# A graph-attention and expert kernel: a wait on GpSimd, a running sum moved off VectorE, filler matmuls and a different set-up

## The chip, the cores and the metric

The kernel runs on one core of one Trainium2 chip. The core's engines are TensorE (PE in the rows; PEld is its weight load), VectorE (DVE), ScalarE (ACT), GpSimd (POOL) and SyncE (SP, which issues the DMAs). The time is device microseconds of one execution; lower is better. Three runs of the kernel before took 2379.27, 2380.46 and 2383.46 us, so the median is 2380.46 us.

## What is computed

The input x is 128 graphs of 128 nodes and 256 features. Layer one is graph attention, layer two a dense mixture of eight experts whose gate is the mean over all graphs:

```python
x = x + gnn(layernorm(x), adj, W, a)
x = x + ffn(layernorm(x), Wr, br, W1, ..., Wo, bo)

# gnn
Wh = h @ W;  s1 = Wh @ a[:256];  s2 = Wh @ a[256:]
e = leaky_relu(s1[:, :, None] + s2[:, None, :], 0.2) + log(adj + 1e-6)
h_prime = softmax(e, axis=-1) @ Wh

# ffn
w = softmax(mean(x, axis=0) @ Wr + br)
h = relu(bn(x @ W1 + b1));  h = relu(bn(h @ W2 + b2));  y = h @ Wo + bo
out = einsum('bfed,fe->bfd', y, w)
```

All of it is fp32; the expert products are three matmuls each on operands split into a high and a low part.

## The kernel before

**Two stages in two blocks.** The graph stage works on G = 32 groups of GB = 4 graphs, one group per step of a software pipeline that every engine walks through in its own loop. In step g, PE projects group g (L716, `project`), the attention of group a = g-1 is computed, and the result x1 of group b = g-2 is formed. The seam is where the graph stage ends and the block of the expert stage begins; the expert stage then runs 256 units (32 tiles by 8 experts) on PE.

**Steps and their kinds.** Steps 0 to 5 and 30 to 33 are written out. Steps 6 to 21 (`layer == 1`) also prepare the W1 weights: in an even step POOL forms four sums in `w_stage` (L451 to L458), in an odd step ACT makes `wq_hi` (L520) and POOL `wq_lo` (L463). Steps 22 to 29 (`layer == 2`) prepare W2: ACT `w_hi` (L532), POOL `w_lo` (L468).

**One step, engine by engine.** DVE: `l_sb` (L621), the row maximum `neg_m` (L628), x1 of group b (L646), the weights p of group a (L658), then eight `bn_stats` (L574, L582). ACT: `s_sb` (L506), its share of the running sum (L514), `wq_hi` in odd steps, `e_sb` (L526), `wh` of group g (L541), which needs POOL's `dev`, then `pT` (L557) and `xnT` (L562). POOL: weight work, its share of the running sum (L476), then `deviations` of the next group (L404 to L424), which needs the `bn_stats` of DVE and whose last instruction is a power that yields `dev`. Each engine executes its list in order.

**The gate's running sum** `acc` (the tile `resb`) adds x1 times its rstd for every group. Of the four graphs of a group h = g-4, DVE adds the two lower (`add_part`, L608); for the two upper ACT writes the scaled copy `x1s_high` (L514) and POOL adds it (L476). There is one `x1s_high` buffer, so ACT's copies of group h wait for POOL's addition of group h-1 (`wait(act, acc_high_done, num(h))`, L512).

**Set-up.** PE transposes the first x tile, forms the column mean of the projection weights `gw` (L694), transposes gw and the vector a (L701, L702), and multiplies them (L708) to append two columns to gw; ACT copies between these steps (L493 to L496). The projection of group 0 waits for that.

**The seam and the end.** `tile_normalise` of tile 0 (L124) stands in step 30 ahead of x1; the three `tile_low` (L162) stand in step 32. In the second block DVE takes the statistics of group 31 (L1029, L1033) and adds groups 30 and 31 to acc (L179). The last tile's output is stored by one DMA of 512 KB (L905).

## Time and profile before

| | us |
|---|---|
| median of three runs | 2380.46 |
| the profiled execution, its own time | 2380.82 |
| its span | 2379.0 |
| set-up to the first `l_sb` (step 1) | 23.19 |
| steps 6 to 21 | 124.90 |
| steps 22 to 29 | 64.03 |
| step 30 to the first matmul of the second block | 29.1 |
| expert stage, first matmul to the end | 2098.7 |

Rows of the timeline give the start, the duration, engine, line, operation, tiles written and read, and in brackets the idle time ahead of the instruction and what ended it. Where several instructions are merged in one row, the duration is that of all. Consecutive instructions overlap a little, so the spacing of starts (called pitch below) says more than a duration.

### The profile page before, as it was taken

The numbers are of one execution on the slowest core, as the hardware profiler recorded it, in microseconds if no ns is written. First come the engines' busy times: TensorE is split into PE (matmuls) and PEld (weight loads), VectorE is DVE, ScalarE is ACT, GpSimd is POOL, SyncE is SP. The second block draws the span as 40 slices with busy tenths as digits, with TensorE's granted clock in tenths as the row PEclk, the third lists the DMA queues.
The fourth block names the chain that finished last, engine by engine and source line by source line (L and its number), as shares of the span: only waits on it lengthen the run. The fifth ranks groups of instructions, "written<-read, shape, count | busy, mean of one in ns | idle before, by whom it ended". The sixth has DMA issues, their size and how long they took to land.

```text
span 2379.0 us, 46022 instructions
## 1 busy us (share of the span) xinstructions
PE 2339.6 (98%) x16164; PEld 2166.8 (91%) x16164; DVE 1687.8 (71%) x2577; ACT 1615.7 (68%) x2524; POOL 435.0 (18%) x566
## 2 busy tenths in 40 slices
PE   8999799999999999999999999999999999999999
PEld 7777689999999999999999999999999999999998
DVE  5999866666776766676666676666666666677666
ACT  5888676666666666666666666666666666666665
POOL 4898621111101011111111101011111111001010
PEclk9999799999999999999999999999999999999999
DMA  5778410000000000000000000000000000000000
GB/s 175 255 251 267 154 36 27 27 26 26 26 26 25 19 9 26 26 26 26 26 26 26 26 26 18 20 14 26 26 26 26 26 26 26 26 26 18 18 10 27
DMA packets 91178, 116.16 MB, mean 49 GB/s; under 512 B 4700, under 2 KB 78856, under 8 KB 91144
## 3 DMA queue, kind: packets, MB, share of 16 engines
q1 hardware_dynamic: 91144, 115.73, 14.8%
q8 instruction: 19, 0.31, 0.1%
q14 instruction: 15, 0.12, 0.0%
HBM read 82.16 MB, written 33.55 MB: 49 GB/s over the span
## 4 chain that ended last, share of the span: by engine, by line
PE 88%; DVE 0%; ACT 0%; issue 0%
PE ps_y L1174 31%; PE ps_wide L171 30%; PE ps_wide L1155 26%; PE ps_t L132 1%; DVE h_lo L1059 0%; DVE z L1052 0%; ACT h_hi L954 0%; ACT v L959 0%; DVE resb L1082 0%; DVE h_lo L1065 0%; DVE z L1042 0%; PE ps_t L1219 0%; PE ps_t L1201 0%; PE ps_t L1206 0%; ACT featT L985 0%
## 5 line engine op out<-in xcount | busy, mean ns | idle before, releaser
L959 ACT ACTIVATE v<-ps_wide,bn_cols 128x256 f32<-128x256 f32 x768 | 434.1, 565 | 375.0 <-PE ps_wide L1155 245.1
L967 ACT ACTIVATE h<-ps_wide,bn_cols 128x512 f32<-128x512 f32 x512 | 399.2, 780 | 314.2 <-PE ps_wide L171 312.0
L1174 PE MATMUL ps_y<-wo_hi,h_hi 128*128 128x256 f32 x2048 | 579.3, 283 | 0.5 <-DVE h_lo L1065 0.5
L1174 PE MATMUL ps_y<-wo_lo,h_hi 128*128 128x256 f32 x2048 | 579.6, 283 | 0.0
L1174 PE MATMUL ps_y<-wo_hi,h_lo 128*128 128x256 f32 x2048 | 579.5, 283 | 0.0
L1059 DVE SCALAR_TENSOR_TENSOR h_lo<-z,h_hi 128x1024 fp32r<-128x1024 f32 x256 | 313.8, 1226 | 341.6 <-ACT h_hi L954 341.6
L1155 PE MATMUL ps_wide<-xq_hi,wq_hi 128*128 128x256 f32 x1792 | 500.9, 279 | 7.4 <-PEq L185 3.1
L1155 PE MATMUL ps_wide<-xq_lo,wq_hi 128*128 128x256 f32 x1792 | 497.8, 278 | 0.0
L1155 PE MATMUL ps_wide<-xq_hi,wq_lo 128*128 128x256 f32 x1792 | 497.0, 277 | 0.0
L171 PE MATMUL ps_wide<-h_hi,w_lo 128*128 128x512 f32 x1024 | 403.9, 394 | 0.0
L171 PE MATMUL ps_wide<-h_lo,w_hi 128*128 128x512 f32 x1024 | 402.0, 393 | 0.0
L171 PE MATMUL ps_wide<-h_hi,w_hi 128*128 128x512 f32 x1024 | 398.3, 389 | 0.5 <-DVE h_lo L1059 0.5
L1174 PEld LDWEIGHTS ps_y<-wo_hi,h_lo 128*128 128x128 f32 x2048 | 392.5, 192 | 0.0
L1174 PEld LDWEIGHTS ps_y<-wo_hi,h_hi 128*128 128x128 f32 x2048 | 390.4, 191 | 1.1 <-DVE h_lo L1065 0.7
L1174 PEld LDWEIGHTS ps_y<-wo_lo,h_hi 128*128 128x128 f32 x2048 | 390.6, 191 | 0.0
L1065 DVE TENSOR_TENSOR h_lo<-h,h_hi 128x1024 fp32r<-128x1024 f32 x256 | 313.5, 1225 | 85.3 <-ACT h_hi L973 82.1
L938 POOL TENSOR_TENSOR resb<-resb,w_bc 128x512 f32<-128x512 f32 x64 | 85.4, 1336 | 1543.4 <-DMA resb<-x_scratch 1537.4
L1155 PEld LDWEIGHTS ps_wide<-xq_hi,wq_hi 128*128 128x128 f32 x1792 | 340.1, 190 | 19.0 <-issue 3.8
L1155 PEld LDWEIGHTS ps_wide<-xq_hi,wq_lo 128*128 128x128 f32 x1792 | 338.4, 189 | 9.8
L1155 PEld LDWEIGHTS ps_wide<-xq_lo,wq_hi 128*128 128x128 f32 x1792 | 338.2, 189 | 0.0
L1082 DVE SCALAR_TENSOR_TENSOR resb<-ps_y,w_node,resb 128x512 f32<-128x512 f32 x448 | 333.3, 744 | 3.9 <-PE ps_y L1174 3.9
L1052 DVE SCALAR_TENSOR_TENSOR z<-ps_wide,bn_cols,v 128x512 f32<-128x512 f32 x256 | 191.9, 750 | 153.4 <-PE ps_wide L1155 145.9
(131 smaller groups left out, 2995.6 us busy)
## 6 DMA issues: line engine op xcount, KB each, us to landing
x_sb<-in_x SPq DMA_DIRECT2D x32, 512.0 KB, 4.0
res<-in_x SPq DMA_DIRECT2D x32, 512.0 KB, 5.9
x1t<-x_scratch SPq DMA_DIRECT2D x32, 512.0 KB, 3.2
resb<-x_scratch SPq DMA_DIRECT2D x32, 512.0 KB, 3.2
out<-resb SPq DMA_DIRECT2D x32, 512.0 KB, 2.9
adj_sb<-in_adj SPq DMA_DIRECT2D x32, 256.0 KB, 6.1
x_scratch<-h SPq DMA_DIRECT2D x16, 512.0 KB, 4.7
x_scratch<-w_bc SPq DMA_DIRECT2D x16, 512.0 KB, 4.9
```

Of the source, the lines that this page charges most:

```text
L132: last = nc.tensor.transpose(ps_x[:, c, b4 * N:(b4 + 1) * N], x1t[:, b4, c * P:(c + 1) * P], ident[:, :])
L171: mm = nc.tensor.matmul(acc_ps, w[:, i, c, cols], s[:, c, :], start=start and n == 0, stop=stop and n == len(terms) - 1)
L938: nc.gpsimd.tensor_tensor(resb[:, g, :], resb[:, g, :], ysum[:, g, :], ALU.add).then_inc(resb_done, 1)
L959: nc.scalar.activation(v[:, slot, :], ps_l1[:, 0, 0:H], ACT.Identity, bias=bn_cols[:, 1, cols], scale=bn_cols[:, 0, cols]).then_inc(done, 1)
L967: nc.scalar.activation(h2[:, m, :], ps_l2[:, m, :], ACT.Relu, bias=bn_cols[:, 3, cols], scale=bn_cols[:, 2, cols]).then_inc(r2_done, 1)
L1052: nc.vector.scalar_tensor_tensor(out=z[:, 0, :], in0=ps_l1[:, 1, :], scalar=bn_cols[:, 0, C * e:C * e + 1], in1=v[:, 0:2, :].rearrange("p ...
L1059: nc.vector.scalar_tensor_tensor(out=h1_lo[:, :, :], in0=z[:, :, :], scalar=0.0, in1=h1_hi[:, :, :].bitcast(F32), op0=ALU.max, op1=ALU.sub ...
L1065: nc.vector.tensor_tensor(h2_lo[u[1] % 2][:, :, :], h2[:, :, :], h2_hi[u[1] % 2][:, :, :].bitcast(F32), ALU.subtract).then_inc(lo2_done, 1)
L1082: nc.vector.scalar_tensor_tensor(out=dst[:, g, :], in0=ps_y[:, g, :], scalar=w_node[:, e:e + 1], in1=old, op0=ALU.mult, op1=ALU.add).then_ ...
L1155: mm = nc.tensor.matmul(out_ps, w[:, e, q, :], x[:, q, :], start=start and n == 0, stop=stop and n == len(terms) - 1, skip_group_check=True)
L1174: mm = nc.tensor.matmul(ps_y[:, b4, :], h[:, c, cols], w[:, e, c, :], start=(k == 0 and b4 % per_bank == 0), stop=(k == len(terms) - 1 and ...
```

## The change

- POOL waits for both halves of p of group a (`p_done`) at the start of each step, ahead of its weight work and its addition.
- The running sum: ACT scales all four graphs of group h into `x1s` (four activations, where there were two), POOL adds 128x1024 in one instruction (128x512 before), DVE's two additions are gone. The order of buffers stays: ACT's copies of group h wait for POOL's addition of h-1 (`acc_done_a`). Groups 30 and 31 are still added by DVE in the second block, now both in `feature_mean`, and their statistics are both taken there.
- `tile_normalise` of tile 0 moves behind p in step 30; the third `tile_low` moves to step 33; `deviations` of step 32 is dropped.
- Set-up: a is loaded broadcast over the partitions; DVE forms gw times a with four accumulating instructions instead of PE's transposes; seven matmuls are issued ahead of the first transpose; an Exp is issued early on ACT.
- Filler matmuls (`keep_clock`): 5 in step 32, 4 in step 33, and 6, 12, 6 and 6 in the first three units of the second block.
- The last tile is stored in two halves.

```diff
                 def step(g, layer):
+                    a = ago(g, 1)
+                    if exists(a):
+                        pool.wait_ge(p_done, 2 * num(a) + 2)
                     if layer == 1 and g[1] == 0:
...
-                        pool.wait_ge(x1s_high_done, num(h) + 1)
-                        wait(pool, acc_high_done, num(h))
-                        nc.gpsimd.tensor_tensor(acc[:, HB:, :], acc[:, HB:, :], x1s_high[:, :, :],
-                                                ALU.add).then_inc(acc_high_done, 1)
+                        pool.wait_ge(x1s_done, num(h) + 1)
+                        pool.wait_ge(acc_set, 1)
+                        wait(pool, acc_done_a, num(h))
+                        nc.gpsimd.tensor_tensor(acc[:, :, :], acc[:, :, :], x1s[:, :, :],
+                                                ALU.add).then_inc(acc_done_a, 1)
...
                         act.wait_ge(dev_done, num(h) + 4)
-                        wait(act, acc_high_done, num(h))
-                        for b4 in range(HB, GB):
-                            last = nc.scalar.activation(x1s_high[:, b4 - HB, :], x1[h[1]][:, b4, :], ACT.Copy,
+                        wait(act, acc_done_a, num(h))
+                        for b4 in range(GB):
+                            last = nc.scalar.activation(x1s[:, b4, :], x1[h[1]][:, b4, :], ACT.Copy,
                                                         scale=rstd_all[:, num(h), b4:b4 + 1])
...
-                    add_part(0)
-                    add_part(1)
...
+                dve.wait_ge(proj_loaded, 2 * 16)
+                for c in range(C):
+                    for k in range(2):
+                        last = nc.vector.scalar_tensor_tensor(
+                            out=x1t[:, 2 * c + k, :], in0=gw[:, c, 0:D], scalar=1.0, in1=a_bc[:, k, :], op0=ALU.mult,
+                            op1=ALU.mult, accum_out=gw[:, c, D + k:D + k + 1])
...
+                    if is_step(g, G):
+                        pe.wait_ge(wh_copied, G)
+                        keep_clock(5)
...
+                    if starts(new, 0) or starts(new, 1) or starts(new, 2):
+                        keep_clock(6)
...
+                    if starts(new, 0):
+                        keep_clock(12)
...
                 def feature_mean():
+                    dve.wait_ge(last_rstd_done, 1)
+                    add_group(G - 2)
                     dve.wait_ge(acc_done, 1)
```

**How the lists read.** POOL in an odd step of the W1 loop, before: the low part of W1, the half addition, the first deviation.

```order
L463 ISA [waits wq_hi_done]
L463 TENSOR_TENSOR wq_lo<-w_stage,wq_hi 128x896
L474 REGISTER_ALU
L476 TENSOR_TENSOR resb<-resb,x1s_high 128x512 [waits acc_high_done,x1s_high_done]
L400 ISA
L402 REGISTER_ALU [waits bnst1]
L404 TENSOR_TENSOR dif<-st 128x8 [waits dev_done,bnst2]
```

The same place in the changed kernel.

```order
L459 ISA [waits wq_hi_done,p_done]
L459 TENSOR_TENSOR wq_lo<-w_stage,wq_hi 128x896
L470 REGISTER_ALU
L473 TENSOR_TENSOR resb<-resb,x1s 128x1024 [waits acc_done_a,acc_set,x1s_done]
L393 ISA
L395 REGISTER_ALU [waits bnst1]
L397 TENSOR_TENSOR dif<-st 128x8 [waits dev_done,bnst2]
```

A wait for p stands ahead of the weight work, and the addition has twice the columns; nothing changed places.

ACT in the same odd step, before: the scaled copies, the high part of W1, the exponentials.

```order
L514 ISA [waits acc_high_done]
L514 ACTIVATE x1s_high<-w_bc,dev 128x256
L514 ISA
L514 ACTIVATE x1s_high<-w_bc,dev 128x256
L519 REGISTER_ALU
L520 ISA [waits wq_sum]
L520 ACTIVATE wq_hi<-w_stage 128x896
L526 ACTIVATE e_sb<-l_sb,neg_m 128x128 [waits p_done,neg_m_done]
```

And in the changed kernel.

```order
L506 ISA [waits acc_done_a]
L506 ACTIVATE x1s<-w_bc,dev 128x256
L506 ISA
L506 ACTIVATE x1s<-w_bc,dev 128x256
L506 ISA
L506 ACTIVATE x1s<-w_bc,dev 128x256
L506 ISA
L506 ACTIVATE x1s<-w_bc,dev 128x256
L511 REGISTER_ALU
L512 ISA [waits wq_sum]
L512 ACTIVATE wq_hi<-w_stage 128x896
L518 ACTIVATE e_sb<-l_sb,neg_m 128x128 [waits p_done,neg_m_done]
```

Four copies now stand between the wait for POOL's addition and the exponentials.

PE in the set-up, before: from the first transposes to the projection of group 0.

```order
L685 MATMUL ps_th<-ident,x_sb 128x128 x7
L694 MATMUL ps_wide<-gw,mean_w 128x256 [waits proj_loaded,mean_w_set]
L694 MATMUL ps_wide<-gw,mean_w 128x256
L701 MATMUL ps_wide<-ident,gw 128x128 [waits gw_centred]
L701 MATMUL ps_wide<-ident,gw 128x128 x3
L702 MATMUL ps_s<-ident,a_rows 128x4
L708 MATMUL ps_s<-a_cols,gwT 128x2 [waits proj_T_copied]
L708 MATMUL ps_s<-a_cols,gwT 128x2 x3
L716 MATMUL ps_wide<-gw,xnT 128x258 [waits xnT_copied,va_copied]
```

And in the changed kernel.

```order
L675 MATMUL ps_th<-ident,x_sb 128x128 x7
L686 MATMUL ps_wide<-gw,mean_w 128x256 [waits proj_loaded]
L686 MATMUL ps_wide<-gw,mean_w 128x256
L691 MATMUL ps_wide<-gw,mean_w 128x2 [waits va_ready]
L691 MATMUL ps_wide<-gw,mean_w 128x2
L704 MATMUL ps_wide<-gw,xnT 128x258 [waits xnT_copied,gw_centred]
```

The transposes of gw and a and the eight small products are gone; two narrow products of the mean stand in their place.

## Rows read from the trace of the kernel before

**Rows 1.** The page: busy time, share of the span and instructions of each engine.

```profile
PE 2339.6 (98%) x16164; PEld 2166.8 (91%) x16164; DVE 1687.8 (71%) x2577; ACT 1615.7 (68%) x2524; POOL 435.0 (18%) x566
```

**Rows 2.** Busy time by stage: stretch, length, busy us of each engine, clock, DMA.

```profile
0.00:23.19 23.19, 15.60 (x68) 12.57 (x69) 3.31 (x9) 7.14 (x16) 5.81 (x23) 1.00 0.42 130
62.25:187.15 124.90, 118.75 (x641) 99.14 (x640) 122.53 (x400) 106.34 (x281) 112.24 (x183) 1.00 0.77 250
187.15:251.18 64.03, 59.05 (x321) 49.88 (x320) 61.74 (x201) 53.73 (x145) 50.48 (x79) 1.00 0.86 279
251.18:280.31 29.13, 19.91 (x94) 15.32 (x93) 27.44 (x80) 17.55 (x46) 22.55 (x39) 0.87 0.33 111
280.31:298.87 18.56, 15.08 (x58) 12.84 (x58) 12.12 (x26) 8.09 (x13) 6.30 (x8) 0.56 0.32 104
```

**Rows 3.** Timeline, DVE, an even and an odd step of the W1 loop.

```profile
114.66 1.38 DVE L582 BATCH_NORM_STATS2 st<-h 128x6 f32<-128x256 f32 x4
115.97 0.86 DVE L608 SCALAR_TENSOR_TENSOR resb<-w_bc,dev,resb 128x256 f32<-128x256 f32 x2
116.75 0.68 DVE L621 SCALAR_TENSOR_TENSOR l_sb<-s_sb 128x512 f32<-128x512 f32 x1
...
119.63 0.28 DVE L658 SCALAR_TENSOR_TENSOR p_sb<-adj_sb,e_sb 128x128 f32<-128x128 f32 x1
...
120.27 0.29 DVE L658 SCALAR_TENSOR_TENSOR p_sb<-adj_sb,e_sb 128x128 f32<-128x128 f32 x1
```

**Rows 4.** Timeline, ACT, the odd step that begins at 116.75.

```profile
116.40 0.95 ACT L514 ACTIVATE x1s_high<-w_bc,dev 128x256 f32<-128x256 f32 x2
117.20 0.99 ACT L520 ACTIVATE wq_hi<-w_stage 128x896 f32 x1
118.19 1.28 ACT L526 ACTIVATE e_sb<-l_sb,neg_m 128x128 f32<-128x128 f32 x4
120.50 1.58 ACT L541 ACTIVATE wh<-ps_wide,dev 128x258 f32<-128x258 f32 x4 [1.04 <-POOL dev L424]
```

**Rows 5.** Timeline, POOL, the same two steps.

```profile
113.81 0.46 POOL L458 TENSOR_TENSOR w_stage<-w_stage 128x128 f32<-128x128 f32 x1
114.23 1.27 POOL L476 TENSOR_TENSOR resb<-resb,x1s_high 128x512 f32<-128x512 f32 x1
116.21 0.30 POOL L404 TENSOR_TENSOR dif<-st 128x8 f32<-128x8 f32 x1 [0.71 <-DVE st L582]
...
118.72 1.65 POOL L424 TENSOR_TENSOR dev<-ve,minus_half 128x8 f32 x1 [0.19 <-POOL ve L420]
120.33 2.17 POOL L463 TENSOR_TENSOR wq_lo<-w_stage,wq_hi 128x896 f32 x1
122.47 1.26 POOL L476 TENSOR_TENSOR resb<-resb,x1s_high 128x512 f32<-128x512 f32 x1
123.70 0.39 POOL L404 TENSOR_TENSOR dif<-st 128x8 f32<-128x8 f32 x1
```

**Rows 6.** Timeline, DVE and POOL in step 31, where p and the addition meet.

```profile
263.94 1.28 POOL L476 TENSOR_TENSOR resb<-resb,x1s_high 128x512 f32<-128x512 f32 x1
...
263.98 1.38 DVE L658 SCALAR_TENSOR_TENSOR p_sb<-adj_sb,e_sb 128x128 f32<-128x128 f32 x1
```

**Rows 7.** Timeline: centring on DVE, projection of group 0, one of a later step.

```profile
8.05 0.69 DVE L587 SCALAR_TENSOR_TENSOR gw<-gw,ps_wide 128x512 f32<-128x512 f32 x1 [8.05 <-PE ps_wide L694]
...
12.99 5.52 PE L716 MATMUL ps_wide<-gw,xnT 128*128 128x258 f32 x16 [0.26 <-ACT gw L496]
...
116.92 3.65 PE L716 MATMUL ps_wide<-gw,xnT 128*128 128x258 f32 x16
```

**Rows 8.** Timeline, step 30: the normalisation on DVE, a small POOL instruction beside it.

```profile
252.50 1.38 DVE L124 TENSOR_SCALAR x1t<-x1t,mean_all,dev 128x256 f32<-128x256 f32 x4
252.60 0.36 POOL L417 TENSOR_TENSOR mean_all<-two_means,half_cols 128x4 f32 x1
```

**Rows 9.** Timeline, the end: the one store of the last tile.

```profile
2375.70 0.40 SPq L905 DMA_DIRECT2D out<-resb  x1
```

168 lines of the change are left out of this document (89 added, 79 removed).

## The prediction

> **What bounds the kernel now.** I read the page first: PE is busy for 98% of the span [rows 1]. That is the expert stage, which the change leaves alone apart from its first three units and its last store. So whatever the change is worth, it is worth in the first 299 us, and there I read the busy time by stage [rows 2]. From step 6 to step 21, the steps that prepare W1, DVE is busy 122.53 us of 124.90, but POOL also 112.24 and ACT 106.34. Eight pairs of steps in 124.90 us make 15.61 us a pair. A full row is not proof of a bound, so I then went through one pair on the timeline to see which wait ends last. In the odd step ACT's wh stands idle for 1.04 us for POOL's dev [rows 4], and POOL itself goes from dev straight on into wq_lo and the addition, with no gap between rows [rows 5]. POOL's only rest in the pair is 0.71 us. So in these steps DVE and POOL share the bound, and work that is taken from DVE and given to POOL is not free.
>
> **What the change buys there.** DVE loses its two additions; they take 0.78 us of a step (start at 115.97, next at 116.75) [rows 3]. The wait for p removes collisions: in step 31 the addition starts at 263.94, and the last p, which elsewhere takes 0.29 us [rows 3], takes 1.38 us, until POOL is done [rows 6]. So a POOL instruction that holds the shared port keeps a two-input DVE instruction out for its whole length, and one such hit costs 1.1 us. Behind p stand bn_stats, which the POOL rows do not disturb (four in 1.38 us beside the addition at 114.23) [rows 3, 5].
>
> [...]
>
> **What it costs there: a loop of waits.** There is one x1s buffer. ACT may copy group h only when POOL has added group h-1. Behind the copies ACT has, in order, wq_hi and then e_sb; e_sb releases p on DVE; and now p releases POOL, which does its weight work and only then the next addition. Before, the last link was missing: POOL took up weight work without p. Now each addition depends on the one before through all of this, once a step. Its links:
> - POOL's end to ACT's start, 0.13 us (dev ends at 120.37, wh starts at 120.50) [rows 4, 5];
> - four copies. Two take 0.80 (116.40 to 117.20) [rows 4], so four take 1.60;
> - wq_hi, odd steps only, 0.99 [rows 4];
> - e_sb 1.28 [rows 4], and 0.10 to DVE (between 0 and the 0.16 that lie between its end and p) [rows 3, 4];
> - p 0.93, from 119.63 to the end of the last at 120.56 [rows 3];
> - DVE to POOL 0.17 (bn_stats end at 116.04, dif starts at 116.21) [rows 3, 5];
> - POOL's weight work: wq_lo 2.14 from start to start [rows 5]; in even steps four sums at a pitch of 0.42 [rows 5], two with a wait for the one before, for which I add 0.13 each: 1.94;
> - the addition of 1024 columns. 512 take 1.23, 896 (wq_lo) take 2.14 [rows 5], 2.37 ns a column between them, so 2.44; doubling gives 2.46.
>
> Odd: 0.13 + 1.60 + 0.99 + 1.28 + 0.10 + 0.93 + 0.17 + 2.14 + 2.44 = 9.78 us. Even: the same without 0.99 and with 1.94 for 2.14, 8.59 us. The pair is 18.37 us against 15.61: +2.76, and over eight pairs +22.1. The first step enters without an addition to wait for by some 0.4 us, so I take **+21.7 us**. l_sb cannot escape: it has two SBUF inputs, and the addition holds the port until its end. The gains above are inside this sum, for it counts p clean and no DVE addition.
>
> [...]
>
> **Steps 22 to 29.** POOL has w_lo there, 512 columns, as long as the old addition, 1.23, and w_hi stands behind e_sb on ACT. The loop is 0.13 + 1.60 + 1.28 + 0.10 + 0.93 + 0.17 + 1.23 + 2.44 = 7.88 us, against 64.03 / 8 = 8.00 [rows 2]. The other chain, dev to wh to xnT to s_sb to l_sb, is about as long; I take **-0.6** (bounds -3 and +1). **Steps 4 and 5** have no weight work, the loop is 6.65, under the 6.9 that DVE needs for a step without its addition (122.53 / 16 - 0.78) [rows 2, 3]: they lose one collision of 1.1 [rows 6] and give 0.1 back, **-1.0**.
>
> **Step 30 to the end of the graph stage.** The normalisation (1.38 us in four instructions) now follows p, where POOL's addition starts. Beside it, before, a POOL instruction of four columns took 0.36 [rows 8], more than the eight-column dif beside DVE's addition, 0.30 [rows 5], so the two do contend. I expect one of the four to run and three to wait the addition out: 2.4 us lost, where 1.1 was lost to a p collision and some 0.3 to DVE's addition. **+1.0** (bounds -1.5, no contention, and +1.5). Behind that POOL has two additions with four copies between, 2.44 + 0.13 + 1.60 + 0.17 + 2.44 = 6.8 us, in place of two half additions and a dropped round of deviations of about 7; but the tile's sums start behind a full addition: **+0.6** (0 to +1.5). Five fillers in step 32 may save that step's slow matmuls; POOL ends later anyway.
>
> **Set-up.** Now the centring ends at 8.74 and the projection starts at 12.99 [rows 7]. Of these 4.25 us a narrow product and a narrow DVE instruction remain, for which I take 0.65 (dif is 0.30 to 0.39, and two signals) [rows 5]: -3.6. The accumulating products fit before the column mean is there at 8.05. The projection takes 5.52 where 3.65 is usual [rows 7]; the earlier matmuls may bring the clock up: between 0 and -1.9, I take the middle. **-4.5** (bounds -2.5 and -6). The cover is the load of a; if its broadcast lands late, that comes off.
>
> **Second block.** [...] Fillers can bring the clock up sooner, but feature_mean now adds two groups in front of unit 1's z: four more instructions at 0.39 [rows 3], +1.6 on DVE's path, which then ends last. **-0.7** (bounds -4, and +2.7 if 24 fillers at 0.26, the mean of 15.08 / 58 [rows 2], fill 3.5 of idle and push the rest). **The last store** takes 3.3 us from its issue to the span's end [rows 9]; half the bytes after the last instruction save **-0.7** (0 to -1.2).
>
> **The sum** is 21.7 - 0.6 - 1.0 + 1.0 + 0.6 - 4.5 - 0.7 - 0.7 = +15.8 us. The profiled execution took 2380.82 us, 0.4 above the median of three. So 2396 us.
>
> **Rivals.**
> - *The loop does not close, POOL's own load decides.* If ACT's copies are never late, POOL's work per pair remains: 1.94 + 2.14 + 4.88 + twice 3.8 for deviations (116.21 to 120.37 is 4.16 [rows 5], less what DVE's addition blocked) = 16.6. +7.6 in place of +21.7: 2382. For it: the copies stand early in ACT's list. Against: the addition ends after they are due.
> - *The port is the whole story (faster).* If l_sb and bn_stats fit around the addition, a step falls toward DVE's own 6.9; I take 7.5, since ACT's list is longer now, so 15.0 a pair: -4.9, all in all 2380.8 - 5.9 - 4.9 = 2370. The place is the addition behind p: it decides once addition and weight work end within the 2.6 us of bn_stats (twice 114.66 to 115.97) [rows 3]. The addition alone fits; with weight work it does not, on rows.
> - *The loop and the losses at the edges*: fillers on a slow clock, the tail's blocked instructions: 2401 to 2403.
>
> **How the numbers follow.** The loop as summed 0.68, the loop with losses 0.10, POOL's load alone 0.12, faster 0.10. The range reaches from the third case's edge, 2382, to 2403. A measurement of this kernel tells about 0.2%, 4.8 us, from no change: faster 0.10, same 0.10, slower 0.80.
>
> **What would show it.** Between step 6's and step 22's l_sb some 146 us in place of 124.90. In an odd step: copies start 0.1 to 0.2 us after an addition ends, e_sb waits for nothing but ACT itself, p starts right behind e_sb, POOL is idle before wq_lo with p as releaser, and l_sb lasts long or starts as the addition ends. Wrong if the addition takes well under 2.3 us, or if the pair stays at 15.6. The set-up is right if the first l_sb starts near 18.7, step 30 if the normalisation's four instructions are stretched to some 3.7 us.

## The result, and where the time is found in the profile after

The changed kernel takes **2436.65 us** (median of 4 runs, 2435.42 to 2439.39) against 2379.94 of the kernel before, measured with it: ratio 1.0237, 95% interval 1.0219 to 1.0255. It is slower by 56.7 us; forecast were 2396 us and a range of 2382 to 2403. The sign was right, the size was not.

Busy time by stage of the changed kernel, with the same borders as [rows 2] (the starts of l_sb in steps 1, 6, 22 and 30, the second block's first product, unit 1's last z). Columns: stretch, length, busy us of PE, PEld, DVE, ACT and POOL with their instructions, granted clock, DMA share, GB/s.

```profile
0.00:17.76 17.76, 13.32 (x73) 11.31 (x74) 5.01 (x18) 6.51 (x14) 5.86 (x22) 1.00 0.65 182
17.76:55.53 37.77, 35.84 (x196) 30.03 (x195) 29.59 (x106) 30.03 (x84) 23.70 (x43) 1.00 0.67 217
55.53:200.29 144.76, 120.40 (x641) 98.77 (x641) 120.09 (x368) 118.13 (x312) 119.00 (x181) 1.00 0.66 216
200.29:268.09 67.80, 60.80 (x321) 49.23 (x321) 55.20 (x184) 59.74 (x160) 56.16 (x81) 1.00 0.81 263
268.09:298.75 30.66, 22.35 (x113) 17.71 (x112) 26.10 (x69) 20.81 (x54) 21.98 (x33) 1.00 0.35 113
298.75:317.65 18.90, 14.49 (x80) 12.49 (x81) 12.85 (x26) 7.99 (x13) 8.56 (x13) 0.86 0.38 118
```

In the profiled executions the span went from 2379.0 to 2433.6 us, +54.6. Stage by stage:

| stage | before | after | difference | the sum had |
|---|---|---|---|---|
| set-up, to step 1's l_sb | 23.19 | 17.76 | -5.4 | -4.5 |
| steps 1 to 6 | 39.06 | 37.77 | -1.3 | -1.0 |
| steps 6 to 22 (W1) | 124.90 | 144.76 | **+19.9** | +21.7 |
| steps 22 to 30 (W2) | 64.03 | 67.80 | **+3.8** | -0.6 |
| step 30 to the second block | 29.16 | 30.66 | +1.5 | +1.6 |
| second block to unit 1's last z | 17.73 | 18.89 | +1.2 | -0.7 |
| from there to the end | 2080.94 | 2115.95 | **+35.0** | -0.7 |

The last line is the surprise: the expert stage, in which the change edits nothing. Here is one tile of its loop, from the first product (one matmul instruction) behind the transposes to the same product of the next tile, first in the kernel before, then in the changed one:

```profile
1030.39:1095.39 65.00, 65.00 (x467) 61.01 (x466) 44.83 (x55) 43.75 (x62) 6.66 (x7) 1.00 0.07 24
```

```profile
1063.26:1129.35 66.09, 66.09 (x468) 61.67 (x465) 44.83 (x55) 43.76 (x62) 6.82 (x7) 1.00 0.07 24
```

Same products, same granted clock (1.00, the upper of the two levels in these traces; the lower is 0.50), PE without a gap in both, DVE and ACT busy as long as before, and yet 1.09 us more per tile. So each product must take longer from start to start. Timeline of PE, a run of 12 products of layer 1 and the first of layer 3, before:

```profile
1023.71 0.28 PE L1155 MATMUL ps_wide<-xq_hi,wq_hi 128*128 128x256 f32 x1
...
1024.96 0.28 PE L1155 MATMUL ps_wide<-xq_lo,wq_hi 128*128 128x256 f32 x1
1025.07 0.28 PE L1174 MATMUL ps_y<-wo_hi,h_hi 128*128 128x256 f32 x1
```

and the same run in the changed kernel:

```profile
1065.48 0.28 PE L1172 MATMUL ps_wide<-xq_hi,wq_hi 128*128 128x256 f32 x1
...
1066.79 0.28 PE L1172 MATMUL ps_wide<-xq_lo,wq_hi 128*128 128x256 f32 x1
1066.91 0.27 PE L1196 MATMUL ps_y<-wo_hi,h_hi 128*128 128x256 f32 x1
```

12 products take 1.36 us before and 1.43 after: 113 against 119 ns. The column of durations (0.28 in both) hides it, since products overlap; only the starts show it. Layers 1, 2 and 3 are the expert's products x W1, h W2 and h Wo. Added up from each product's start to the next one's, and averaged over the tiles of the loop in whose records nothing is missing, the time of a tile by layer is:

| us a tile | layer 1 (168 products, 256 columns) | layer 2 (96, 512 columns) | layer 3 (192, 256 columns) | period |
|---|---|---|---|---|
| before | 19.20 | 21.97 | 23.03 | 65.00 |
| after | 20.09 | 22.38 | 22.84 | 66.09 |

Before, layer 1 is at 113 ns product after product (at 118 in part of the unit behind the transposes). After, it runs through a cycle: 122, 120, 119, 115, 117, 122, 120, ... Behind the first few tiles the same figures recur in every tile, to within a nanosecond. (The transposes and a few small products make up the other 0.79 us of the period, in both kernels.)

**The loop of waits in W1.** Two steps of the changed kernel, l_sb at 145.31 and 154.63: POOL, ACT and DVE apart.

```profile
144.30 2.36 POOL L473 TENSOR_TENSOR resb<-resb,x1s 128x1024 f32<-128x1024 f32 x1
...
151.29 0.46 POOL L447 TENSOR_TENSOR w_stage<-w_stage 128x128 f32<-128x128 f32 x1 [0.98 <-DVE p_sb L642]
...
153.20 2.36 POOL L473 TENSOR_TENSOR resb<-resb,x1s 128x1024 f32<-128x1024 f32 x1
...
160.59 2.10 POOL L459 TENSOR_TENSOR wq_lo<-w_stage,wq_hi 128x896 f32 x1 [1.37 <-DVE p_sb L642]
162.64 2.35 POOL L473 TENSOR_TENSOR resb<-resb,x1s 128x1024 f32<-128x1024 f32 x1
```

```profile
146.87 1.71 ACT L506 ACTIVATE x1s<-h,dev 128x256 f32<-128x256 f32 x4 [1.68 <-POOL resb L473]
148.48 1.26 ACT L518 ACTIVATE e_sb<-l_sb,neg_m 128x128 f32<-128x128 f32 x4
...
155.71 1.71 ACT L506 ACTIVATE x1s<-w_bc,dev 128x256 f32<-128x256 f32 x4 [1.11 <-POOL resb L473]
157.32 0.94 ACT L512 ACTIVATE wq_hi<-w_stage 128x896 f32 x1
158.16 1.26 ACT L518 ACTIVATE e_sb<-l_sb,neg_m 128x128 f32<-128x128 f32 x4
```

```profile
145.31 1.90 DVE L611 SCALAR_TENSOR_TENSOR l_sb<-s_sb 128x512 f32<-128x512 f32 x1 [0.64 <-ACT s_sb L498]
...
148.61 1.66 DVE L630 SCALAR_TENSOR_TENSOR h<-ps_th,rinv,res 128x256 f32<-128x256 f32 x4 [0.67 <-ACT x1s L506]
150.19 0.28 DVE L642 SCALAR_TENSOR_TENSOR p_sb<-adj_sb,e_sb 128x128 f32<-128x128 f32 x1
...
159.45 0.29 DVE L642 SCALAR_TENSOR_TENSOR p_sb<-adj_sb,e_sb 128x128 f32<-128x128 f32 x1 [0.24 <-ACT e_sb L518]
```

The loop closes as forecast: the copies wait 1.68 and 1.11 us for POOL's addition, POOL waits 0.98 and 1.37 us for p, and works through its weight work before the next addition. From step to step l_sb starts 9.31 and 9.01 us apart, 18.32 a pair (forecast: 18.37). One link is not in the forecast: x1 (L630) waits 0.67 us for the copies, "<-ACT x1s". In the odd round p starts behind e_sb (0.24 us of waiting). In the even one it starts behind x1, at 150.19, when e_sb has been done since 149.74: there the path goes through x1 and not through e_sb.

### The profile page after: what moved, and what is told of

It reads as the page before. It is cut to its first block, busy times and chain, and to the rows that moved or that the text cites. A ratio compares the mean times of both kernels' runs of the same rounds, so it can differ in the third digit from the quotient of the medians.

```text
span 2433.6 us, 46080 instructions
## 1 busy us (share of the span) xinstructions
PE 2378.8 (98%) x16217; PEld 2188.9 (90%) x16217; DVE 1677.2 (69%) x2522; ACT 1638.5 (67%) x2582; POOL 450.7 (19%) x562
## 4 chain that ended last, share of the span: by engine, by line
PE 88%; POOL 3%; DVE 3%; ACT 2%; issue 2%; DMA 0%; ACTq 0%; DVEq 0%; POOLq 0%; SPq 0%
PE ps_y L1196 30%; PE ps_wide L168 29%; PE ps_wide L1172 26%; POOL resb L473 2%; ACT x1s L506 1%; PE ps_t L129 1%; DVE p_sb L642 1%; DVE st L566 1%; PE ps_wide L704 1%; DVE h L630 0%; ACT e_sb L518 0%; PE ps_th L721 0%; ACT wq_hi L512 0%; DVE w_bc L630 0%; DMA w_stage<-in_L_ffn_Wo 0%
## 5 line engine op out<-in xcount | busy, mean ns | idle before, releaser
L1172 PE MATMUL ps_wide<-xq_hi,wq_hi 128*128 128x256 f32 x1792 | 510.4, 285 | 7.1 <-DVE z L1058 3.4
L1172 PE MATMUL ps_wide<-xq_hi,wq_lo 128*128 128x256 f32 x1792 | 506.5, 283 | 0.0
L1172 PE MATMUL ps_wide<-xq_lo,wq_hi 128*128 128x256 f32 x1792 | 506.2, 282 | 0.0
L168 PE MATMUL ps_wide<-h_hi,w_hi 128*128 128x512 f32 x1024 | 404.5, 395 | 0.6 <-DVE h_lo L1075 0.6
L1172 PEld LDWEIGHTS ps_wide<-xq_hi,wq_hi 128*128 128x128 f32 x1792 | 340.1, 190 | 19.4 <-DVE z L1058 4.1
```

The source lines that it names most:

```text
L168: mm = nc.tensor.matmul(acc_ps, w[:, i, c, cols], s[:, c, :], start=start and n == 0, stop=stop and n == len(terms) - 1)
L1172: mm = nc.tensor.matmul(out_ps, w[:, e, q, :], x[:, q, :], start=start and n == 0, stop=stop and n == len(terms) - 1, skip_group_check=True)
```

## The experiments

The first question is the expert stage. In the changed kernel ones_cols is gone, last_st has grown and last_mv is gone. All that is allocated behind them lies elsewhere: by the author's estimate wq and w 32 bytes lower, w_bc, h2, x1t, xs and xq 32 bytes higher, h1, h2_hi, h2_lo and wo 192 bytes higher. No profile shows an address, and how much room a buffer of 16 bytes takes was not shown: the places in bytes, here and in the expectations, are that estimate, made from the sizes of the buffers. The first theory is that these places cost the time. The rival is something else in the changed program.

**Moving buffers only.** The edit of `a1_before_off64` to the kernel before (nothing reads or writes the three buffers; by the estimate wq, w and xq then lie against a multiple of 64 bytes as they do in the changed kernel):

```diff
+        pad_w = sb("pad_w", [P, GB])
         wq_hi = sb("wq_hi", [P, E, Q, P], F32R)
...
+            pad_a = sba("pad_a", [P, GB])
             bn_rows = sba("bn_rows", [EC, 2, 5, P])
...
+            pad_b = sbb("pad_b", [P, GB])
             last_ve = sbb("last_ve", [P, GB])
```

> [...] Theory A (the start address of an operand costs TensorE time): the tile period rises from 65.00 to about 66.1 us and the whole by 30 to 34 us, to about 2412. Theory B (something else in the changed kernel, such as where its instructions lie, makes the expert stage slower): period 65.0, time 2380. No theory expects a change before step 32.

Measured: 2411.25 us (2410.14 to 2412.49), ratio 1.0131, interval 1.0114 to 1.0148. Period 65.99, and the graph stage is the same (W1 124.75, second block at 279.89). So 31 us come from the places of buffers alone.

`a2_after_on64` puts the same three lines into the changed kernel (pad_b ahead of last_dif):

> The changed kernel with nothing changed but the same three unused buffers, so that wq, w, xq, h1 and wo all start on multiples of 64 bytes again, as in the kernel before. Theory A: the tile period falls from 66.09 to 65.0 us and the whole to about 2404, which leaves +24 us from the first 320 us. Theory B: 66.1 and 2437.

Measured: 2436.58 us, ratio 1.0240 (1.0223 to 1.0257), period 66.11. No time came back. Either theory A was wrong in the changed kernel, or a multiple of 64 is not the condition.

`a3_after_weights_on64` has the changed kernel with

```diff
+        pad_w = sb("pad_w", [P, GB])
         wq_hi = sb("wq_hi", [P, E, Q, P], F32R)
...
+        pad_s = sb("pad_s", [P, GB])
         last_st = sb("last_st", [P, 2, GB, 6])
```

> The changed kernel with one unused buffer ahead of wq_hi and one ahead of last_st: the weights wq and w start on multiples of 64 bytes, w_bc, h2, resb, x1t, xs and xq stay 32 bytes off. Layer 2 (weights w, activations h1, which are aligned in both kernels) slowed down too, from 228.8 to 232.9 ns, so within theory A the weights are the likelier side: period 65.0, time about 2404. If it is the streamed activations alone: period about 65.4 to 66.1. Theory B: 66.1 and 2437.

and `a4_after_acts_on64` with

```diff
+        pad_x = sb("pad_x", [P, GB])
         w_bc = sb("w_bc", [P, E, P])
```

beside pad_a and pad_b:

> The changed kernel with one unused buffer ahead of w_bc (and the two at the starts of stage A's and the second block's buffers): w_bc, h2, resb, x1t, xs and xq start on multiples of 64 bytes, the weights wq and w stay 32 bytes off. Theory A with the weights as the side that counts: period 66.1, time 2437. With the streamed activations: layer 1 fast again, about 65.4 (the 144 products of 120 columns by 5 ns less) and 2414, layer 2 as slow as in the changed kernel. Theory B: 66.1 and 2437.

Measured: a3 2420.81 us (ratio 1.0175), a4 2437.52 us (1.0245). In a3 layer 2 is back at 21.96 us a tile, layer 1 still at 20.00; a4 moved little (20.01 and 22.52). a4 (66.15 us a tile) came out as forecast for the weights as the side that counts, and for theory B; a3 (65.63) as forecast for the streamed side alone. No one theory fitted both, so the next kernel put everything back.

**The changed kernel with its buffers where they were.**

```diff
+        pad_w = sb("pad_w", [P, GB])
         wq_hi = sb("wq_hi", [P, E, Q, P], F32R)
...
-        last_st = sb("last_st", [P, 2, GB, 6])
+        pad_s = sb("pad_s", [P, 32])
...
         xq_lo = sb("xq_lo", [P, Q, H], F32R)
+        last_st = sb("last_st", [P, 2, GB, 6])
...
+            pad_a = sba("pad_a", [P, 88])
...
+            pad_b = sbb("pad_b", [P, 40])
```

> The changed kernel with its buffers put back where the kernel before has them: wq, w, w_stage, w_bc, h2, resb, x1t, xs and xq at exactly the same addresses (an unused buffer of 16 bytes where ones_cols was, one of 128 bytes where last_st and last_mv were, last_st itself behind xq_lo), h1, h2_hi, h2_lo and wo of the second block 512 bytes above theirs, stage A's x_sb, xnT and p_sb at theirs. Theory A2 (TensorE's pitch depends on where the operands lie, by more than a multiple of 64): layer 1 again at a constant 113 ns, period 65.00, time 2403 to 2405. Theory B (something else of the changed kernel makes the expert stage slower, and the moved buffers of the first four runs only added to that): period 66 and 2434 to 2438. Steps 6 to 22 stay at 144.8 us by both.

Measured: **2400.76 us** (2400.59 to 2402.93), ratio 1.0092 (1.0075 to 1.0109). W1 is 144.77 us, and one tile is

```profile
1051.06:1116.06 65.00, 65.00 (x467) 61.01 (x466) 44.84 (x55) 43.75 (x62) 6.57 (x7) 1.00 0.07 24
```

as before, with the three layers at 19.20, 21.97 and 23.03 us. That settles it: 36 us of the 57 come from where the buffers lie, and none of these from the program's instructions. What is left, 20.7 us, is the change proper.

`b2_before_acts_64_up` moves, in the kernel before, xq and its neighbours by 64 bytes (pad_x of 16 columns ahead of w_bc, pad_a and pad_b of 112):

> The kernel before with the weights in place and w_bc, h2, resb, x1t, xs and xq 64 bytes higher (still multiples of 64, but no longer of 128); the second block's buffers 512 bytes higher. If the multiple of 128 of the streamed xq, or its distance from wq, is what keeps layer 1 at 113 ns: layer 1 rises to 118 to 120 ns, the period by 0.8 to 1.0 us (168 products by 5 to 6 ns), the time to 2404 to 2410. If only the multiple of 64 counts: 65.00 and 2380.

Measured: 2414.67 us, ratio 1.0150 (1.0133 to 1.0167), period 66.11, with the three layers at 20.08, 22.21 and 23.03 us, the very figures of a2. By the sizes of the buffers the two kernels agree in where wq, w and xq lie, and in h1, h2 and wo to a multiple of 256 bytes: the same places, two different programs, the same pitches. The kernel before lost 35 us because xq and the buffers allocated with it moved by 64 bytes, from one multiple of 64 to the next. (The second block's buffers moved by 512 bytes as well, as they did in b1, which lost nothing by it.) Layer 2 rose by 0.24 us a tile although neither w nor h1 moved against a multiple of 512: a layer's pitch is not decided by its own operands alone.

**The products alone.** `m1_places_alone` has TensorE with nothing beside it:

```diff
+            def product(bank, w, x, n, start, stop):
+                return nc.tensor.matmul(ps[:, bank, 0:n], wa[:, w:w + P], xa[:, x:x + n], start=start, stop=stop)
+
+            def layer_1(sw, sx, k):
+                for q in range(k):
+                    r = q % 7
+                    for w, x in ((0, 0), (7168, 0), (0, 1792)):
+                        last = product(0, sw + w + 128 * r, sx + x + 256 * r, 256, True, True)
+                return last
...
+            for kind, k in ((layer_1, 16), (layer_3, 16), (layer_2, 10)):
+                for order in (range(16), range(15, -1, -1)):
+                    for i in order:
+                        last = kind(8 * (i // 4), 8 * (i % 4), k)
```

> Leaves the whole computation out: it writes zeros, and only measures TensorE's pitch. After 100 products to warm up, three kinds of products run with nothing else on the chip's core: layer 1's pattern (256 streamed columns, hi and lo parts as far apart as in the kernel: 28672 and 7168 bytes), layer 3's (256 columns; stationary parts 8192 bytes apart, streamed ones 16384) and layer 2's (512 columns; 16384 and 4096), each with the stationary operand 0, 32, 64 or 96 bytes past a multiple of 128 and the streamed one likewise: 16 cells of 48 products (30 for layer 2), in rising and then in falling order. Theory A (TensorE's own reads, by where the operands lie): layer 1's pattern takes 113 ns at stationary 64 and streamed 0 and 118 to 120 at 64/64, 32/32, 96/32 and 64/96, as in the kernels so far; other cells may be fast too, and layer 3's cell 0/0 takes 120. Theory C (the places matter only because ScalarE and VectorE read and write other buffers beside it): all cells alike, within 1 ns.

The stationary operand is the one of 128 columns, which PEld's instructions load (128x128 each, 0.19 us in the kernel before), the streamed one that of 256 or 512 columns. Three stretches of this kernel with 48 products each and one with 30 (the counts include neighbours that reach in; here there is no DVE column). They are layer 1's pattern at stationary/streamed 0/0, 64/0 in rising order and 64/0 in falling order, then layer 2's at 0/0:

```profile
37.72:43.48 5.76, 5.76 (x51) 5.76 (x49) 0.00 (x0) 0.00 (x0) 1.00 0.00 0
83.28:88.73 5.45, 5.45 (x50) 5.45 (x49) 0.00 (x0) 0.00 (x0) 1.00 0.00 0
168.43:174.09 5.66, 5.66 (x51) 5.66 (x49) 0.00 (x0) 0.00 (x0) 1.00 0.01 3
401.69:408.52 6.83, 6.83 (x33) 5.64 (x31) 0.00 (x0) 0.00 (x0) 1.00 0.00 0
```

5.76 / 48 is 120.0 ns, 5.45 / 48 is 113.5, 5.66 / 48 is 117.9. The tables have the mean of the second half of each cell, in ns, from one execution (rising order; for layer 1's pattern the falling order stands in brackets where it is more than 0.5 off):

| layer 1's pattern | streamed 0 | 32 | 64 | 96 |
|---|---|---|---|---|
| stationary 0 | 120.0 | 117.8 (120.0) | 117.8 | 120.0 |
| 32 | 118.3 | 120.0 | 117.7 (116.7) | 117.8 |
| 64 | **113.3 (117.8)** | 118.3 | 120.0 | 117.8 (116.7) |
| 96 | 118.8 | 117.8 | 118.3 | 120.0 |

| layer 2's pattern | streamed 0 | 32 | 64 | 96 |
|---|---|---|---|---|
| stationary 0 | 226.7 | 233.3 | 228.9 | 233.3 |
| 32 | 233.4 | 226.7 | 233.2 | 228.9 |
| 64 | 233.3 | 233.2 | 226.7 | 233.2 |
| 96 | 234.3 | 233.3 | 233.2 | 226.7 |

Theory C is out: the effect is there with ACT and DVE idle. Two things are to be seen. The figure depends on how the two operands lie to each other: equal places give 120.0 with 256 columns and 226.7 with 512, whichever place it is. And four cells of layer 1's pattern have two figures, one in each order, the widest apart 113.3 and 117.8 at 64/0: what ran before a cell counts too. Layer 3's pattern gave the same table as layer 1's, within 0.1 ns.

The remainders modulo 128 do not fix the figure. In layer 2's table 64/0 and 0/64 are as far apart modulo 128, and take 233.3 and 228.9 ns. The kernel before has w and h1 at 64/0 and takes 228.9. Worked out from the sizes of the buffers, w's start less h1's is 192 more than a multiple of 256 bytes there, as it is in the cells 0/64 and 32/96, and 64 more in 64/0 and 96/32. The distance modulo 256 gives the right figure for layer 2 in before, a1, a3 and the changed kernel (228.9, 233.2, 228.8 and 233.1 ns measured), and misses it in a2 and b2 (231.4 for 228.9) and by 1 ns in a4, where what ran before may count. For layer 1 the cells do not cover the changed kernel: its wq and xq are 128 apart modulo 256, and no cell is.

**The gate's running sum.** All of these have b1's places, so that the tile period is 65.00 us in each of them and the difference lies ahead of the expert loop. `c1_pool_free_of_p` takes the wait out:

```diff
                 def step(g, layer):
-                    a = ago(g, 1)
-                    if exists(a):
-                        pool.wait_ge(p_done, 2 * num(a) + 2)
                     if layer == 1 and g[1] == 0:
```

> As b1_after_at_before_places, but POOL does not wait for p at the start of a step. Theory of the loop (addition, copies, e_sb, p, weight work, addition): its last link is gone, so POOL's own load decides, 16.6 us a pair by the prediction's sum (weight work 1.94 and 2.14, additions 4.72 in all, deviations twice 3.8); with l_sb or p shut out by additions that now start at any time up to 17.6. Steps 6 to 22: 133 to 141 us in place of 144.8. Steps 22 to 30: 62 to 67.8. Theory that the additions alone are the cost, wherever they start: 144.8 and no change. The expert stage as in b1.

Measured: 2445.43 us (2441.91 to 2448.12), ratio 1.0272, so **45 us slower** than b1. Steps 6 to 22 take 176.80 us and 22 to 30 79.82. Both theories failed, and the timeline says why; POOL and DVE of one odd step:

```profile
161.71 2.08 POOL L459 TENSOR_TENSOR wq_lo<-w_stage,wq_hi 128x896 f32 x1
163.74 2.39 POOL L473 TENSOR_TENSOR resb<-resb,x1s 128x1024 f32<-128x1024 f32 x1
```

```profile
162.00 1.93 DVE L642 SCALAR_TENSOR_TENSOR p_sb<-adj_sb,e_sb 128x128 f32<-128x128 f32 x1 [0.23 <-ACT e_sb L518]
...
163.86 2.42 DVE L642 SCALAR_TENSOR_TENSOR p_sb<-adj_sb,e_sb 128x128 f32<-128x128 f32 x1
...
166.21 0.28 DVE L642 SCALAR_TENSOR_TENSOR p_sb<-adj_sb,e_sb 128x128 f32<-128x128 f32 x1
```

The first p waits wq_lo out; before the second comes, the addition has started (163.74), and that one waits it out too: 1.93 + 2.42 us for two instructions of 0.28. An odd step takes 13.0 us, an even one 9.3. PE is left without work for longer, and its mean granted clock in the stretch is 0.88, part of it at the lower level (0.50). That this adds to the loss is not shown: the odd steps take 12.6 to 13.0 us all through, and the two stretched p alone (3.8 us) account for the 3.7 us by which they are longer than b1's 9.3. So with the full addition POOL's wait for p is a help, not a harm. In these rows POOL and DVE take turns by whole instructions. What they contend for was not shown: the shared port of the prediction and of the expectations is the author's name for it.

`c2_two_x1s` gives the copies two buffers in turn:

```diff
-            x1s = sba("x1s", [P, GB, D])
+            x1s = [sba(f"x1s{i}", [P, GB, D]) for i in range(2)]
...
-                        wait(act, acc_done_a, num(h))
+                        wait(act, acc_done_a, num(h) - 1)
```

> As b1_after_at_before_places, with two x1s buffers in turn, so that ACT's copies wait for the addition before the last and not for the last. Theory of the loop: the link from the addition to the copies is gone; what is left is DVE's own 6.9 us a step plus the 1.3 to 1.9 us for which an addition keeps l_sb out, and POOL's own 8.2: 16.4 to 17.4 us a pair, steps 6 to 22 131 to 139 us. If DVE's shut port is the whole cost and the copies' wait only happens to end at the same time: 18.3 a pair, 144.8.

Measured: 2387.36 us (2385.95 to 2389.34), ratio 1.0031 (1.0019 to 1.0044), 13.4 us less than b1. The pair is 17.06 us, steps 6 to 22 135.16, 22 to 30 64.50. In this kernel the copies start while the addition runs:

```profile
141.18 2.36 POOL L476 TENSOR_TENSOR resb<-resb,x1s 128x1024 f32<-128x1024 f32 x1
142.23 1.77 ACT L509 ACTIVATE x1s<-h,dev 128x256 f32<-128x256 f32 x4
```

The loop of waits is confirmed by cutting it: one link taken out, 9.6 us back in W1 and 3.2 in W2. Some 7 us above the kernel before stay.

`d2_half_sum_waits_for_p` takes the kernel before's running sum (two graphs on DVE, two on POOL) into b1 and leaves all the rest:

```diff
+                    if with_acc:
+                        dve.wait_ge(dev_done, num(h) + 4)
+                        dve.wait_ge(acc_set, 1)
+                        wait(dve, acc_low_done, num(h))
+                        for b4 in range(HB):
+                            part = nc.vector.scalar_tensor_tensor(out=acc[:, b4, :], in0=x1[h[1]][:, b4, :],
+                                                                  scalar=rstd_all[:, num(h), b4:b4 + 1],
+                                                                  in1=acc[:, b4, :], op0=ALU.mult, op1=ALU.add)
+                        part.then_inc(acc_low_done, 1)
...
-                        nc.gpsimd.tensor_tensor(acc[:, :, :], acc[:, :, :], x1s[:, :, :],
+                        nc.gpsimd.tensor_tensor(acc[:, HB:, :], acc[:, HB:, :], x1s_high[:, :, :],
                                                 ALU.add).then_inc(acc_done_a, 1)
...
-                        for b4 in range(GB):
+                        for b4 in range(HB, GB):
```

> As b1_after_at_before_places, but the gate's running sum as in the kernel before: two graphs of each group on DVE (0.78 us a step), two copied on ACT and added on POOL (512 columns); POOL still waits for p, and set-up, fillers, normalisation and last store are the changed kernel's. Theory of the loop: from the measured 9.31 (odd) and 9.01 us (even) two copies (0.86) and half an addition (1.13) go, which leaves 7.3 and 7.0, under DVE's own 7.65 a step; DVE is the bound and p is clean: 15.2 to 15.6 us a pair, steps 6 to 22 121.5 to 125 us, steps 22 to 30 61 to 64; time 2372 to 2378. If POOL's wait for p is the harm and not the full addition: above 130 us, time over 2385.

and `d3_half_sum_free` is that without POOL's wait (the diff of c1):

> As d2_half_sum_waits_for_p without POOL's wait for p, so the kernel before with the short set-up, the fillers, the moved normalisation and the halved last store. With the full addition the missing wait cost 32 us in steps 6 to 22, because wq_lo and the addition each took the port between two of the four p. With the half addition the kernel before shows 124.90: 124 to 130 us here, steps 22 to 30 64 to 66, time 2374 to 2383. If the wait costs more than it saves with the half addition, d3 is below d2 in these steps.

Measured: d2 **2372.88 us** (2371.37 to 2375.47, 7 runs), ratio 0.9970 (0.9959 to 0.9982); d3 2379.27 us (2374.54 to 2382.08, 10 runs), ratio 0.9996 (0.9986 to 1.0006). d2 beats both kernels, the one before by 0.3%. Its time is as expected for the loop; its stretches missed theirs a little, W1 with 125.72 us (121.5 to 125 expected), W2 with 60.41 (61 to 64). Steps 22 to 30 of d2, then of d3:

```profile
181.92:242.33 60.41, 57.96 (x321) 49.73 (x320) 58.36 (x202) 52.96 (x145) 49.72 (x83) 1.00 0.90 293
```

```profile
183.44:247.45 64.01, 59.00 (x321) 49.92 (x320) 61.73 (x200) 53.73 (x145) 50.45 (x79) 1.00 0.86 279
```

The wait for p buys 3.6 us here, 7.55 against 8.00 us a step. In W1 it buys nothing (125.72 against 124.91), and between step 30 and the second block it costs 1.0 us (28.63 against 27.58). In W1 the addition, moved off p, meets DVE's own additions instead (row below, of d2; the two take 0.86 where POOL leaves them alone [rows 3]). The two profiled executions are 3.3 us apart, 1.3 of it in the set-up, the medians 6.4: d3's ten runs spread over 7.5 us, and no trace shows the rest.

```profile
148.61 1.27 POOL L477 TENSOR_TENSOR resb<-resb,x1s_high 128x512 f32<-128x512 f32 x1
148.90 1.66 DVE L615 SCALAR_TENSOR_TENSOR resb<-h,dev,resb 128x256 f32<-128x256 f32 x2
```

**Can the other layers have better places?** Three kernels on d2, the edits being unused buffers in the second block: ahead of h1_hi 192 bytes, of wo_hi 64 (`e1`); ahead of h2_hi0 192, of wo_hi 64 (`e2`); ahead of h1_hi 192, of h2_hi0 320 (`e3`). For e1:

```diff
+            pad_h1 = sbb("pad_h1", [P, 48])
             h1_hi = sbb("h1_hi", [P, C, T], F32R)
...
+            pad_wo = sbb("pad_wo", [P, 16])
             wo_hi = sbb("wo_hi", [P, E, C, D], F32R)
```

> As d2_half_sum_waits_for_p with two unused buffers in the second block, 192 bytes ahead of h1_hi and 64 bytes ahead of wo_hi. Layer 3 then has stationary h2 and streamed wo as far apart modulo 128 (64) and modulo 256 as layer 1 has wq and xq, layer 2 has w and h1 equal modulo 128. By the cells of m1_places_alone: layer 3 falls from 120 to 113 ns where it stays in the fast state, 117.8 where not (192 products a tile: 1.3 or 0.4 us), layer 2 from 228.9 to 226.7 (96 products, 0.2 us). Period 63.5 to 64.4 us, time 2373 less 20 to 47: 2326 to 2353. If the places count only one product at a time and layer 3 is held by something else: 65.0 and 2373.

> As d2_half_sum_waits_for_p with 192 unused bytes ahead of h2_hi0 and 64 ahead of wo_hi: layer 3's places as in e1_all_three_layers, h1 where it is in the kernel before. Layer 3 as in e1, layer 2 228.9 ns as before: period 63.7 to 64.6, time 2332 to 2360. Theory that the state carries over from one layer's products to the next (the cells differed between rising and falling order): layer 1 or 2 may change too, although none of its operands moved.

> As d2_half_sum_waits_for_p with 192 unused bytes ahead of h1_hi and 320 ahead of h2_hi0: layer 2's w and h1 are equal modulo 128 (226.7 ns in m1_places_alone), h2 and wo keep their places modulo 512. Layer 2 from 228.9 to 226.7, period 64.8, time 2366 to 2368, layers 1 and 3 unchanged at 113 and 120. Theory of the carried state: layer 1, which comes behind layer 2, leaves its 113 ns and the gain is lost or turned.

| | us | ratio to before | layer 1, us a tile | layer 2 | layer 3 | period |
|---|---|---|---|---|---|---|
| d2 | 2372.88 | 0.9970 | 19.20 | 21.97 | 23.03 | 65.00 |
| e1 | 2384.27 | 1.0015 (1.0005 to 1.0025) | 19.80 | 22.05 | 22.51 | 65.15 |
| e2 | 2383.27 | 1.0012 (1.0002 to 1.0021) | 19.88 | 22.01 | 22.61 | 65.26 |
| e3 | 2377.00 | 0.9988 (0.9978 to 0.9997) | 19.33 | 21.96 | 22.99 | 65.07 |

All three missed the gain and came out slower than d2 by their medians; for e3 (4 us, of which its period explains 2) the interval still touches d2's. The execution of e1 that was profiled was the fastest of its ten, 6 us under their median, so its layers may be a best case. Layer 3 fell from 120 to 117 to 118 ns, the dearer of its cell's two figures, and layer 1, none of whose operands moved in e2, went from 113 to 118. In e3 only layer 2's operands moved against each other. The layer 1 products right behind it take 118 on average, those behind the next run of layer 3 113 again. Layer 2 itself did not gain: of its runs of 12 products the first six take 231 ns and the next six 227, so they average 228.8 where the cell, in its second half, showed 226.7. So the pitch is carried over from one layer to the next, and runs as short as the kernel's (3 to 12 products) need not reach the figure of a cell. What inside TensorE does this is not shown by these runs, and a layout in which all three layers are at their best figure was not found.

**The second block.** `f1_no_fillers_block_2` is d2 without the two keep_clock lines of the second block:

```diff
-                    if starts(new, 0) or starts(new, 1) or starts(new, 2):
-                        keep_clock(6)
...
-                    if starts(new, 0):
-                        keep_clock(12)
```

> As d2_half_sum_waits_for_p without the fillers of the second block's first three units (30 products whose result nothing reads). From the second block's first product to unit 1's z took 18.9 us with them and 17.7 before, with DVE's eight additions of feature_mean and its sum last. Theory that DVE's path ends last: still 18.9, and the time within 1 us of d2's 2372.9. Theory that the fillers themselves push it: 17.7 or less, time 1 to 3 us less. Theory that they hold the clock up: the products behind run at the lower level and the time is 1 to 4 us more.

Measured: 2375.79 us (2371.68 to 2377.97), ratio 0.9980 (0.9970 to 0.9989), an interval that overlaps d2's. From the block's first product to unit 1's last z it takes 19.06 us against d2's 18.99: the fillers do not touch that path. Twenty units in, f1 is 1.2 us behind (175.03 against 173.81 us from the block's first product). Some 17 us into the block the clock fell to its lower level (0.50), for 10.2 us in f1 (289.54 to 299.78) and for 6.8 us in d2 (287.87 to 294.70). The two profiled executions are 2.6 us apart; the rest of that lies ahead of the second block, where f1's set-up ended 1.5 us later (see the set-up below). So the 2.9 us between the medians are not all the fillers' worth.

## Why the prediction missed, point by point

**The step that failed** stands in its first lines: the expert stage is what "the change leaves alone apart from its first three units and its last store", so that "whatever the change is worth, it is worth in the first 299 us". The sum therefore has nothing for the tiles of the expert stage. The change leaves their instructions alone, but not their operands' places. The stage behind unit 1 took 35.0 us more, where the sum had -0.7. a1 and b2 (only places changed: +31 and +35 us) and b1 (places restored: 2400.76) put 36 us on it. Without that step's miss the forecast of 2396 stood 5 us from b1, and b1 lies in the range. That nearness is in part luck, since terms missed both ways, as follows. Nothing in the forecast had a rival for the places, although the full diff shows one buffer deleted and one grown ahead of most others. Why a place costs what it does stays open.

**The loop in W1: the mechanism right, the sum near by luck**, +19.9 for +21.7, 18.32 us a pair for 18.37. c2 shows the mechanism by cutting the loop, d2 by halving it. But the halves missed in opposite directions. From one addition's end to the next the even round took 8.90 us (146.66 to 155.56) for 8.59, because it goes through x1, 1.58 us, where the sum had e_sb and 0.10, 1.38, and because the copies reach x1 1.74 us after their start, for 1.60. The odd round took 9.43 us for 9.78: wq_hi 0.84 for 0.99, e_sb to p 1.29 for 1.38, wq_lo 2.05 for 2.14, the addition 2.35 for 2.44. The rest of the 1.8 is the entry: the first step, from 55.53 to 62.94, took 7.4 us, since it came in without an addition to wait for. The rival "POOL's own load" is out (18.3, not 16.6), and so is the faster one; with the half sum POOL's wait does not bring a step to 7.5 us in W1 either (7.86).

**W2: the term was mis-sized**, +3.8 for -0.6, 8.35 us a step for 7.88 (and 9.32 in the first, which still has W1's work behind it). The sum went from the copies through e_sb to p. One step of the changed kernel, POOL, ACT and DVE:

```profile
239.82 1.28 POOL L464 TENSOR_TENSOR w_lo<-w_stage,w_hi 128x512 f32 x1 [1.10 <-DVE p_sb L642]
241.06 2.36 POOL L473 TENSOR_TENSOR resb<-resb,x1s 128x1024 f32<-128x1024 f32 x1
...
248.19 1.28 POOL L464 TENSOR_TENSOR w_lo<-w_stage,w_hi 128x512 f32 x1 [1.11 <-DVE p_sb L642]
```

```profile
243.57 1.71 ACT L506 ACTIVATE x1s<-w_bc,dev 128x256 f32<-128x256 f32 x4 [0.57 <-POOL resb L473]
245.18 1.26 ACT L518 ACTIVATE e_sb<-l_sb,neg_m 128x128 f32<-128x128 f32 x4
```

```profile
245.42 1.66 DVE L630 SCALAR_TENSOR_TENSOR w_bc<-ps_th,rinv,res 128x256 f32<-128x256 f32 x4 [0.73 <-ACT x1s L506]
246.99 0.28 DVE L642 SCALAR_TENSOR_TENSOR p_sb<-adj_sb,e_sb 128x128 f32<-128x128 f32 x1
```

e_sb is done at 246.44 and p starts at 246.99, behind x1. x1 waits for the copies, since they read the buffer that it is to overwrite: w_lo 1.24 + addition 2.31 + 0.20 + copies 1.71 + 0.14 + x1 1.57 + p 0.92 + 0.28 is 8.37, the time from w_lo to w_lo. That wait stood in the diff (x1s_done, where it was x1s_high_done); in the kernel before, none of the 128 x1 instructions waited. It is the same miss as in W1's even round, with no odd round to hide it.

**Steps 1 to 6**: -1.3 for -1.0. Steps 4 and 5 gave 1.2, as forecast; steps 1 (-1.0) and 3 (+0.9), which the sum did not have, cancelled.

**Step 30: right in kind and size.** The four instructions of the normalisation, beside the addition from 273.02 to 275.49:

```profile
272.86 3.42 DVE L121 TENSOR_SCALAR x1t<-x1t,mean_all,dev 128x256 f32<-128x256 f32 x4
```

3.42 for 1.38 [rows 8], 2.0 us lost where 2.4 were forecast, and the step is +1.46 for +1.0. What follows up to the second block, for which the sum had +0.6, came to nothing (+0.04).

**Set-up: right in kind, its size in part luck**, -5.4 for -4.5. The projection started at 9.32 us, for 12.99, and took 3.75 us, not 5.52 [rows 7]: at that time the clock was at its upper level (1.00). The forecast had taken the middle of that term. Other executions of the same set-up did not get it. Here are the products of the projection that start before 12.00 us, in the changed kernel and in f1:

```profile
9.32 2.88 PE L704 MATMUL ps_wide<-gw,xnT 128*128 128x258 f32 x12 [0.25 <-DVE gw L593]
```

```profile
9.50 2.84 PE L719 MATMUL ps_wide<-gw,xnT 128*128 128x258 f32 x6 [0.25 <-DVE gw L597]
```

Twelve products in the time of six: in f1 the clock fell to its lower level at 9.65 and rose at 13.06 (granted 0.50 between them), and the whole projection took 5.44 us. Of the 13 profiled executions with the new set-up, eight had 3.75 or 3.76 us here and step 1's l_sb at 17.7 to 18.1; five (c1, c2, d3, e2, f1) had 5.3 to 5.9 and l_sb at 19.4 to 20.8. With the old set-up it stood at 21.5 to 23.2. So the seven early matmuls did not secure the clock. The cover held but for the last piece: DVE waits for the broadcast.

```profile
6.94 0.42 DVE L583 SCALAR_TENSOR_TENSOR x1t<-gw,a_bc 128x256 f32<-128x256 f32 x1 [1.22 <-DMA a_bc<-in_L_gnn_a]
```

**The second block: wrong sign**, +1.2 for -0.7. The forecast saw that feature_mean would end last but let the warmer clock win. The clock did rise (0.86 for 0.56 [rows 2]), but unit 1's first z stood behind DVE:

```profile
309.98 1.66 DVE L176 SCALAR_TENSOR_TENSOR resb<-h,dev,resb 128x256 f32<-128x256 f32 x4
311.67 1.67 DVE L176 SCALAR_TENSOR_TENSOR resb<-w_bc,dev,resb 128x256 f32<-128x256 f32 x4
...
313.45 1.92 DVE L1109 TENSOR_REDUCE feat_sum<-resb 128x256 f32<-128x1024 f32 x1
...
315.81 0.74 DVE L1058 SCALAR_TENSOR_TENSOR z<-ps_wide,bn_cols,v 128x512 f32<-128x512 f32 x1
```

Eight additions stand there where there were four (the other four stood at the block's start, ahead of unit 0's z, where DVE then idled 2.45 us). The first z started 17.06 us into the block, for 15.25 before: +1.8, near the +1.6 of the forecast. Only between the two z of unit 1 did anything come back: the last one waited 0.46 us for PE, for 1.08 before. f1 agrees that the fillers are without effect up to here, and shows them worth 1.2 us behind it.

**The last store: right**, -0.8 for -0.7: its second half is issued at 2431.08 and the span ends at 2433.6, 2.5 us for 3.3 [rows 9].

## What to carry to other kernels

Deleting a buffer is an edit to every buffer behind it. Where TensorE is the bound, compare the addresses of its operands before and after, and their distances (here modulo 256), and read the starts of consecutive products, not their durations; a pad of a few bytes is part of a tuned kernel. Before work is handed to an engine that takes longer over it (512 columns of the sum: 1.26 us on POOL [rows 5], 0.86 on DVE [rows 3]), write down the loop of waits that its buffer closes: a single buffer for the hand-over tied three engines into one chain here, a second one gave 13 us back. Follow everything that waits for its writers, too: the wait of x1 for the copies was the part of the chain that the forecast lacked. And where the rows show two engines taking turns, as POOL and DVE do here, count a collision as the whole length of the other's instruction (p took 1.93 and 2.42 us for 0.28), once for each instruction that can slip in between: the wait that keeps them apart was worth 45 us in b1 against c1.
